# Lookahead units hoisted to the head of the chunk loop, second-layernorm loads and transposes waited for in groups

## What is computed

```python
x = x + attn(layernorm(x), Wq, Wk, Wv, Wg, Wo, gamma, beta)
x = x + ffn(layernorm(x), w_gate, w_up, w_down)

# attn: 16 heads of 64, gated linear recurrence
q, k, v = heads(x @ Wq.T), heads(x @ Wk.T), heads(x @ Wv.T)
a = sigmoid(heads(x @ Wg.T))
h_t = a_t[..., None] * h_{t-1} + k_t[..., None] * v_t[..., None, :]
y_t = q_t @ h_t
return (layernorm(y) * gamma + beta) @ Wo.T

# ffn: hidden 3072, int weights / 127
return (silu(x @ wg.T) * (x @ wu.T)) @ wd.T
```

## Time and profile before

| | us |
|---|---|
| median of 2 runs (1480.50 and 1481.44) | 1480.97 |
| the profiled execution, its own time | 1471.82 |
| its span, slowest core (core 2) | 1470.3 |
| spans of the 8 cores | 1457.9 to 1470.3 |
| granted TensorE clock, mean of each core | 0.820 to 0.826 |
| attention phase and weight loads, core 2, to the last x2d store issue | 0 to 818 |
| second layernorm, to the issue of the `s_wd` load | 818 to 913 |
| `s_wd` and first `s_wgu` loads, PE idle | 913 to 962 |
| gate and up matmuls, then the down projection | 962 to 1470 |

### The profile page before, as it was taken

How to read it: one execution, slowest core, us unless ns; L and a number is a source line. 1 busy time by engine, 2 the same in 40 slices (tenths; PEclk the granted TensorE clock), 3 DMA queues, 4 the chain that set the end, 5 groups by cost and what they waited for, 6 DMA issues and landing times.

```text
span 1470.3 us, 17695 instructions; the slowest of 8 cores (1457.9 to 1470.3 us)
## 1 busy us (share of the span) xinstructions
PE 930.8 (63%) x5815; PEld 446.4 (30%) x5892; DVE 513.4 (35%) x928; ACT 330.7 (22%) x691; POOL 136.0 (9%) x193
## 2 busy tenths in 40 slices
PE   0034375756765586666744000089999999999997
PEld 0002232333323332432332000034444444444443
DVE  0022325456645674556566344011221221211010
ACT  0031722533163316322122122011111111100000
POOL 2000000010101010110011001011111111100110
PEclk9977577767976788678866555589999999999999
DMA  9903120121212220311012355944424434312322
GB/s 143 176 2 101 27 74 0 30 73 58 101 24 53 69 115 15 59 68 62 1 45 86 96 128 132 174 43 43 44 29 44 43 30 43 44 56 88 115 86 100
DMA packets 144456, 99.97 MB, mean 68 GB/s; under 512 B 123504, under 2 KB 123504, under 8 KB 144368
## 3 DMA queue, kind: packets, MB, share of 16 engines
q0 software_dynamic: 72816, 81.02, 26.4%
q1 hardware_dynamic: 71552, 17.83, 6.4%
HBM read 93.86 MB, written 16.78 MB: 75 GB/s over the span
## 4 chain that ended last, share of the span: by engine, by line
PE 52%; DVE 20%; DMA 10%; issue 5%; ACT 5%; another core or an unknown queue 5%; DVEq 1%; SPq 1%; ACTq 0%; POOL 0%; POOLq 0%
PE p_g L907 11%; PE p_d L946 11%; PE p_u L920 11%; PE p_fr L339 5%; DMA s_x2T<-s_a 4%; DVE s_nL L360 3%; DVE s_nL L435 3%; DMA s_wd<-wdi 3%; PE p_py L475 3%; DVE s_ht L667 2%; DVE s_y L731 2%; PE p_fr L475 2%; PE p_pp L575 2%; PE p_py L406 2%
## 5 line engine op out<-in xcount | busy, mean ns | idle before, releaser
L907 PE MATMUL p_g<-s_x2T,s_wgu 128*128 128x512 bf16 x753 | 181.4, 381 | 150.9 <-DMA s_wgu<-wui 150.1
L920 PE MATMUL p_u<-s_x2T,s_wgu 128*128 128x512 bf16 x752 | 179.9, 379 | 0.8
L926 DVE SCALAR_TENSOR_TENSOR s_hff<-p_u,s_act 128x512 bf16<-128x512 f32 x96 | 66.4, 691 | 291.1 <-PE p_u L920 262.1
L946 PE MATMUL p_d<-s_wd,s_hff 128*128 128x512 bf16 x753 | 165.1, 379 | 2.0 <-DVE s_hff L926 1.2
L907 PEld LDWEIGHTS p_g<-s_x2T,s_wgu 128*128 128x128 bf16 x768 | 75.4, 98 | 241.9 <-issue 152.2
L339 PE MATMUL p_fr<-s_xlnT,s_wg 128*128 128x512 bf16 (+1 forms) x312 | 79.8, 417 | 67.4 <-DMA s_xlnT<-s_xln 59.5
L913 ACT ACTIVATE s_act<-p_g 128x512 f32<-128x512 f32 x96 | 57.3, 597 | 270.1 <-PE p_g L907 270.1
L946 PEld LDWEIGHTS p_d<-s_wd,s_hff 128*128 128x128 bf16 x768 | 75.1, 98 | 92.0 <-issue 1.7
L920 PEld LDWEIGHTS p_u<-s_x2T,s_wgu 128*128 128x128 bf16 x768 | 75.1, 98 | 90.6
L575 PE MATMUL p_pp<-s_wo,s_E 128*128 128x512 bf16 x250 | 72.6, 455 | 25.5 <-DVE s_xr L600 23.5
L705 PE MATMUL p_py<-s_V,s_P 64*64 64x64 bf16 x256 | 29.8, 237 | 89.9 <-DVE s_P L641 89.9
(11 more groups left out here) (109 smaller groups left out, 1128.3 us busy)
## 6 DMA issues: line engine op xcount, KB each, us to landing
s_x<-x2d POOLq DMA_DIRECT2D x32, 512.0 KB, 4.8
s_x<-xs POOLq DMA_DIRECT2D x18, 512.0 KB, 7.5
s_xr<-xs POOLq DMA_DIRECT2D x16, 512.0 KB, 3.9
x2d<-s_xr POOLq DMA_DIRECT2D x16, 512.0 KB, 2.9
out<-s_x POOLq DMA_DIRECT2D x16, 512.0 KB, 3.0
s_wd<-wdi POOLq DMA_DIRECT2D x1, 6144.0 KB, 41.8
s_wgu<-wgi POOLq DMA_DIRECT2D x24, 256.0 KB, 4.3
s_wgu<-wui POOLq DMA_DIRECT2D x24, 256.0 KB, 5.4
```

Source lines behind the costliest of these rows:

```text
L907: addD("t", lambda t, buf=buf, t4=t4, j=j, pb=pb: t.matmul(p_g[pb][:], s_wgu[buf][:, TILE * j:TILE * (j + 1)], s_x2T[:, 2048 * j + 512 * t ...
L920: addD("t", lambda t, buf=buf, t4=t4, j=j, pb=pb: t.matmul(p_u[pb][:], s_wgu[buf][:, 1024 + TILE * j:1024 + TILE * (j + 1)], s_x2T[:, 2048 ...
L926: addD("v", lambda v, hc=hc, t4=t4, pb=pb: v.scalar_tensor_tensor(s_hff[:, 2048 * hc + 512 * t4:2048 * hc + 512 * (t4 + 1)], p_u[pb][:], S ...
L946: addD("t", lambda t, ts=ts, buf=buf, hf=hf, hcc=hcc: t.matmul(p_d[buf][:, 512 * hf:512 * (hf + 1)], s_hff[:, 2048 * hcc + TILE * ts:2048 ...
```

## The change

Three edits. In `emit_loop` the first 5 units of the next group (four `u_tile`, one `u_xt`) are called right behind `splice.loads()`, ahead of the chunk loop, and the tables are set to [0, 4, 4, 0] and [4, 4]. In the second layernorm the loads are issued in pairs: at an even tile both the load of `tt` and that of `tt + 1`, each with the wait it had, and the semaphore count after both is what both tiles' readers wait for. Last, the transposes' epoch is closed only every fourth tile, and quarter `t4` of the gate matmuls waits for the count of its own four transposes instead of for all 16.

```diff
@@ emit_loop
         if splice:
             splice.loads()
+            for _ in range(min(5, len(splice) - 9)):
+                splice.pop(0)()
@@
-                    sched = {4: [5, 4, 4, 0], 2: [6, 7]}[npair]
+                    sched = {4: [0, 4, 4, 0], 2: [4, 4]}[npair]
@@
-                sched = {2: [6, 7]}[npair]
+                sched = {2: [4, 4]}[npair]
@@ second layernorm
     a2_done = {}
+    ln2q = {}
     for tt in range(16 if TRUNC == 0 else 0):
         buf = tt % 2
-        dmaD("g", GX, lambda g, tt=tt, buf=buf: g.dma_start(
-            out=s_x2[:, 1024 * buf:1024 * (buf + 1)],
-            in_=x2d.ap()[TILE * tt:TILE * (tt + 1), :]),
-            wait=([(VE, a2_done[tt - 2])] if tt >= 2 else []))
-        ld = O.close_epoch(GX)
+        if tt % 2 == 0:
+            for t2 in (tt, tt + 1):
+                dmaD("g", GX, lambda g, t2=t2: g.dma_start(
+                    out=s_x2[:, 1024 * (t2 % 2):1024 * (t2 % 2 + 1)],
+                    in_=x2d.ap()[TILE * t2:TILE * (t2 + 1), :]),
+                    wait=([(VE, a2_done[t2 - 2])] if t2 >= 2 else []))
+            ld_pair = O.close_epoch(GX)
+        ld = ld_pair
@@ after the transpose of s_a2
-        O.close_epoch(ST)
+        if tt % 4 == 3:
+            ln2q[tt // 4] = O.close_epoch(ST)
@@ gate matmuls
-            w0 = [(GQ, gu_ld), (ST, ln2_tp), (SE, silu_of.get(pb, 0))]
+            w0 = [(GQ, gu_ld), (ST, ln2q.get(t4, ln2_tp)),
+                  (SE, silu_of.get(pb, 0))]
```

## The result

The changed kernel is slower by 1.1%: ratio 1.011 with a 95% interval of 1.0082 to 1.0138, about 16 us, and within the 2% that counts as no change. The medians over all runs are 1485.24 us before and 1500.47 us after; they include some disturbed executions, which the ratio leaves out. Measured again beside the experiments the same kernel gave 1.0167 (1.0131 to 1.0203), about 25 us. The profiled execution took 1501.71 us, against 1471.82 before.

The account below looks back on a forecast made before the run. PE's wait for `s_wgu`, behind the second layernorm and the `s_wd` load, was taken as the bound; 27.0 + 2.0 - 0.7 = 28.3 us on 1480.97 gave 1509.3, range 1500 to 1515.

Parts of the forecast that it names:

- The forecast's own range: Whole kernel: 1505 to 1514 us around the predicted median 1509.3, given a chance of 0.80.
- the first rival: Second layernorm: paired loads land as fast as one alone, so only 18.7 us slower, 1499.7; chance 0.10 for this or near it.
- The loads in pairs: Second layernorm: six even tiles ahead of the `s_wd` load cost 4.50 us more each, tile 0 2.0; sum 29.0.
- The rival of loads as fast as alone: Second layernorm: each exposed paired load takes 3.4 us, not 5.0, giving 18.7 us slower; chance 0.10 for this or near it.
- The gate: Gate matmuls after the second layernorm: waiting per quarter removes a wait that doesn't end last, since `s_wgu` lands later; worth 0.
- The tail of the transposes: End of second layernorm: last transpose hidden with 11 us slack; as a rival it becomes the bound, 1514 to 1517, chance 0.07.
- Warm-up loop, -0.7: PE in the warm-up loop: state matmuls behind three more gate blocks may run at the higher clock, saving 0.7 us.
- The hoisted units on ACT: Layernorms of the moved units: ACT's order is unchanged, so they start as before and the line 339 wait stays; 0.
- The hoisted units on SP: Groups' loops: four transposes leave ahead of the first of `s_y`, delaying nothing and gaining nothing for pair 1's gate matmuls; 0.

Follow-up runs that it names:

- pair_only: The kernel before with only the paired loads of the second layernorm added, no hoisting, gate as before; ratio 1.0196, 29 us slower.
- single_buf: The kernel before with one half of `s_x2` for all tiles, so each load leaves only when the tile before is written; ratio 1.0478, 70 us slower.
- hoist_gate: The changed kernel with the paired loads undone, keeping the hoisted units and the gate per quarter; ratio 0.9966 to the kernel before, 5 us faster.
- warm_reorder: The kernel before with only 4 and 4 gate blocks in the warm-up loop instead of 1 and 7; ratio 0.9999.
- hoist_only: The kernel before with only the hoisted units and both new tables; ratio 0.9938, 9 us faster.
- hoist_groups: The kernel before with the hoisted units, but PE's warm-up order kept at 1 and 7 gate blocks; ratio 0.9952.

## Why the prediction was right or wrong

The time, 1500.47, lies inside the range of 1500 to 1515 and the direction is right, but that it lies inside is in part luck. The sum was too high, 28.3 us against 16 and 25 in two measurements, and the kernel before came out at 1485.24, 4.3 us above the 1480.97 that the forecast started from; 16 us on that would be 1497. The forecast's own range, 1505 to 1514, was missed, and the value lies at the first rival's 1499.7, for another reason than the rival's. By its own steps:

- *The loads in pairs, 29.0.* Right in mechanism and in size: pair_only measures 29. On the slowest core the six even tiles ahead of `s_wd` take 10.54 on average (forecast 10.69) and the odd ones 6.03 (6.19); tile 0's first reduction comes 5.04 after the first issue instead of 3.56, so 1.5 for a forecast of 2.0. Together that is 26.4 on this core, and 27.8 to 29.0 for the stage in the mean over 8 cores. The rival of loads as fast as alone is refuted by single_buf and by the 4.9 us of the changed kernel's own loads.
- *The gate, 0.* Right: hoist_gate isn't faster than hoist_only. The reason named, POOL's order, is right as well; with `s_wd` moved the same gate is worth 7 to 9 us in the profiles and 6 in the timed runs.
- *The tail of the transposes.* The slack held. With X for the end of tile 13's write (937.7), the last transpose left at 968.3 and took 15.8, so it landed at X + 46.4 for a forecast of 47.6, and PE's first gate matmul came at X + 53.0.
- *Warm-up loop, -0.7.* Not seen, and too small to be: warm_reorder is at 0.9999, with 1.4 us either way.
- *The hoisted units on ACT, 0.* Right: in the warm-up loop the wait ahead of line 339 is no shorter, 27.4 to 31.3 us on the 8 cores for 27.4 to 29.6 before.
- *The hoisted units on SP, 0.* This is the step that failed. "The gate matmuls of pair 1 began at 457.76, behind PE's own order, so earlier transposes gain nothing there" took a start for a cause. The gate matmuls waited 1.61 us for the last of the transposes. The numbers stood in the earlier trace rows: 449.19 + 6.25 = 455.4 is only the end of the issues, and with a landing of 2.8 behind it 457.76 is too close to call it free. Its price is 5 to 9 us over three loops (hoist_only, hoist_groups and hoist_gate), of which the waits themselves are 5.9 on core 2 and 4.1 in the mean over 8 cores; the rest is the shorter time to the Wo matmuls, read as the clock's, and the spread of the runs.

29 less 7, the middle of that, is 22, which lies between the two measurements. The profiled pair of executions alone would have hidden this error: it shows +29.9, because the profiled execution of before, at 1471.8, lies below all of that kernel's timed runs beside the result (from 1478.1).

## What to carry to other kernels

When two loads share a count, ask when the later one may leave, not when the earlier one does: a pair needed buffers for two pairs here, or the prefetch was gone. When a call is moved, follow each queue to the landing of its last DMA and compare that with the consumer's start; an idle time of 1 or 2 us put down to an engine that isn't in the wait list was a DMA here. And the large load moved off the path stalled the small ones behind it on the same queue; splitting it is the next thing to try, which no run here did.

## What was unexpected

A gap of 1.6 us ahead of a block of 32 matmuls went with a mean granted clock of 0.74 instead of 0.82 in that block, and with 0.7 us beyond itself. And two loads of 256 KB issued 12 and 13 us behind a load of 6 MB on the same queue took 35.2 and 38.2 us to land: the large one took 48.3 us from 939.54, so to 987.8, and the small ones landed 1 us ahead of it and 3 us behind it. How the queue shares its bandwidth between them isn't shown.
